# Four chained attention layers on 16 by 16 images: a new order of the stages in all four engine queues

## The chip, the core and the metric

The kernel runs on one core of a Trainium2 chip. TensorE (PE) multiplies and transposes, VectorE (DVE), ScalarE (ACT) and GpSimd (POOL) work elementwise, SyncE (SP) issues transfers. Each engine takes its own queue in program order and waits for the others by semaphores. The metric is device microseconds of one launch.

## What is computed

The input `x` has 2 batches of 128 channels of 16 by 16 pixels (N = 256), in float32. Four layers follow one another; batches never mix. Cut to what matters:

```python
# layer 0: group norm, attention over pixels
hn = group_norm(x); q, k, v = wq@hn + bq, wk@hn + bk, wv@hn + bv
x = wp @ (softmax(q.T @ k * C**-0.5) applied to v) + bp + x
# layer 1: position attention, then channel attention
pam = gamma_pam * (softmax(q.T @ k) applied to v) + x
x = gamma_cam * softmax(max(cen) - cen) @ pam + pam      # cen = pam @ pam.T
# layer 2: 8 heads of 16, with a fixed embedding added to q and k
x = softmax(q.T @ k / 4) applied to v, @ Wout + bout + x
# layer 3: linear attention and feed-forward, norms over channels
f = chan_ln(x) * norm_g
q, k, v = [dwconv3x3(w @ f, dw) for each]
q = softmax(q, over the 16 of a head) * 16**-0.5; k = softmax(k, over pixels)
o = silu(q applied to (k @ v.T));  x = chan_ln(out_w @ o) * out_norm_g + x
x = ff_w2 @ (chan_ln(gelu(ff_w1 @ chan_ln(x))) * ff_g2) + x
```

## The kernel before

Everything stays in SBUF once loaded; a batch is one tile of 128 channels by 256 pixels, and where pixels must stand on the partitions it is two tiles of 128 (NT = 2). Each engine's program is a list of stages, small functions that take the batch `b`, called in an order written out by hand. Within layer 0 and 1 batch `b` uses PSUM banks 4b to 4b+3.

Layers 0 and 1: TensorE computes `q0_product`, `k0_product`, `scores0`, VectorE `max0`, ScalarE `exps0`, TensorE `p0_transposes`, `scale0` (it spreads the reciprocal sums of `sums0` over the partitions), `mix0`, and VectorE `x1_sum`. Layer 1 repeats this (`qk1_product`, `scores1`, ... `pam_sum`) and goes on with `pam_transposes`, `energy`, `energy_min`, `energy_exp`, `ce_transpose`, `co_product` and `x2_sum`. Between them lie products on the weights alone: `wg_mean` and VectorE's `centre_wg` make `wgc`, from which GpSimd makes the convolution's weights; `ff_mean_1`, `ff_mean_2` and `centre_ff_1`, `centre_ff_2` do the same for the feed-forward. `keep_clock(n, dst)` issues n products of zeros that nothing reads.

Layer 2 works in four groups (two per batch, `grp` 0 to 3) of four heads. For each: `group_scores` (TensorE, into four banks), `group_max` (VectorE, four reductions of 128 by 512), `max_transposes`, `shift_add`, `group_scores_T` (the scores again, transposed, with the maxima subtracted), four `head_exp` (ScalarE), `group_mix`, `mixed_evac`, `mixed_transposes`, `o2_norm`. Per batch `o2_transposes`, `o2_evac` and `x3_tokens` end the layer.

Layer 3, per batch: `x3_stats` (VectorE), a root, `f_scale`, `f_transposes`, `f_evac` and `shift_edges` (ScalarE, three shifted copies of f). From there three ways run side by side. The q way is 18 products `conv(j, first, last)` on TensorE (j is the half of the pixels, first to last the taps), then `q_max`, `q_exp`, `q_norm`, `q_transposes`. The k way is `k_1x1`, nine taps on VectorE (`k_taps_0`, `_3`, ...) and their maximum, `k_exp`, `ek_transposes`. The v way is `v_1x1`, nine scaled copies on ScalarE (`v_products`), eight additions on GpSimd (`v_sums`, line 251), each of which waits for the one two ahead of it or more, so that they run one behind the other, and `v_transposes`, `v3_evac`. Then `ctx_product`, `context`, `o3_product`, `o3_tanh`, `silu`, `y_products` (two products in one stage), `y_stats`, root 4, `x4_sum`, `x4_stats`, `x4_transposes`, `x4_evac`, `h_products`, root 5, `gelu`, `h_stats`, `h_transposes`, `hT_evac`, `ff_product`, root 6, `y_sum`, `y_transposes`, `y_evac`. All inverse roots (`root3` to `root6`, line 213) are made on GpSimd, in the same queue as the value sums. In the tail the order alternates: a stage of batch 0, one of batch 1 further ahead in the chain.

Of the kernel before, what the change touches and what calls it, by code (L numbers as in the profile page):

```python
# [4 lines left out]
NB = 2  # L5
# [3 lines left out]
NT = N // 128  # L9
# [33 lines left out]
def build(nc, x, pack_a, pack_b, pack_c, taps, out):  # L43
# [5 lines left out]
    with ExitStack() as ctx:  # L49
# [147 lines left out]
        def _(pool):  # L197
# [62 lines left out]
        def _(act):  # L260
# [63 lines left out]
            for stage, b in ((k0_evac, 0), (k0_evac, 1), (exps0, 0), (exps0, 1), (v0_evac, 0), (rb0_evac, 0), (v0_evac, 1), (p0T_evac, 1),  # L324
                             (rb0_evac, 1), (k1_evac, 0), (v1_evac, 0), (k1_evac, 1), (exps1, 0), (exps1, 1), (v1_evac, 1), (rb1_evac, 0),
                             (p1T_evac, 1), (rb1_evac, 1), (pamT_evac, 0), (pamT_evac, 1), (energy_exp, 0), (energy_exp, 1), (outwg_evac, 0)):
                stage(b)
# [116 lines left out]
            for stage, b in ((k2_evac, 0), (k2_evac, 1), (v2_evac, 0), (v2_evac, 1)):  # L444
                stage(b)
            for grp in range(NB * NG):
                for i in range(HG):
                    head_exp(HG * grp + i)
                    if i == 1 and 0 < grp <= NG:
                        mixed_evac(0, grp - 1)  # L450
            mixed_evac(1, 0)
            x3T_evac(0)
            mixed_evac(1, 1)
            f_scale(0)
            f_evac(0)
            o2_evac(1)
            for stage, b in ((shift_edges, 0), (v_products(0, 4), 0), (x3T_evac, 1), (f_scale, 1), (v_products(4, 6), 0), (f_evac, 1),
                             (shift_edges, 1), (v_products(6, TAPS), 0), (k_exp, 0), (v_products(0, 3), 1), (q_exp, 0),
                             (v_products(3, TAPS), 1), (ekT_evac, 0), (qT_evac, 0), (v3_evac, 0),
                             (k_exp, 1), (o3_tanh, 0), (q_exp, 1), (gelu_table, 1), (ekT_evac, 1), (x4_evac, 0), (qT_evac, 1), (v3_evac, 1),  # L460
                             (o3_tanh, 1), (gelu, 0), (hT_evac, 0), (x4_evac, 1), (gelu, 1), (y_evac, 0), (hT_evac, 1), (y_evac, 1)):
                stage(b)
# [3 lines left out]
        def _(dve):  # L466
# [196 lines left out]
            for stage, b in ((q0_evac, 0), (q0_evac, 1), (xb0_sum, 0), (xb0_sum, 1), (max0, 0), (max0, 1), (sums0, 0), (p0T_evac, 0),  # L663
                             (sums0, 1), (centre_outw, 0), (x1_sum, 0), (x1_sum, 1), (q1_evac, 0), (q1_evac, 1), (centre_wg, 0), (max1, 0), (max1, 1),
                             (xb1_sum, 0), (xb1_sum, 1), (sums1, 0), (p1T_evac, 0), (sums1, 1),
                             (pam_sum, 0), (pam_sum, 1),
                             (half_masks, 0), (centre_ff_1, 0), (energy_min, 0), (ce_scale, 0), (energy_min, 1), (ceT_evac, 0), (centre_ff_2, 0),
                             (ce_scale, 1), (ceT_evac, 1), (x2_sum, 0), (x2_sum, 1)):
                stage(b)
# [48 lines left out]
            def k_taps(b, first=0, last=TAPS):  # L718
# [121 lines left out]
            for stage, b in ((k_taps_0, 0), (x3_stats, 1), (k_taps_3, 0), (k_taps_6, 0), (k_taps_8, 0), (k_taps_0, 1), (q_max, 0), (k_sums, 0),  # L840
                             (k_taps_3, 1), (q_norm, 0), (k_taps_6, 1), (context, 0), (k_taps_8, 1), (q_max, 1), (silu, 0), (q_norm, 1),
                             (y_stats, 0), (k_sums, 1), (x4_sum, 0), (x4_stats, 0), (context, 1), (silu, 1), (h_stats, 0), (y_stats, 1),
                             (y_sum, 0), (x4_sum, 1), (x4_stats, 1), (h_stats, 1), (y_sum, 1)):
                stage(b)
# [3 lines left out]
        def _(pe):  # L848
# [103 lines left out]
            def keep_before_qk1(b):  # L952
                pe.wait_ge(s["rb0_d"], 1)
                keep_clock(1, bank[1])

# [78 lines left out]
            for stage, b in ((q0_product, 0), (k0_product, 0), (q0_product, 1), (k0_product, 1), (scores0, 0), (scores0, 1),  # L1034
                             (v0_product, 0), (v0_product, 1), (p0_transposes, 0), (scale0, 0), (p0_transposes, 1), (scale0, 1), (mix0, 0),
                             (mix0, 1),
                             (wg_mean, 0), (keep_before_qk1, 0), (qk1_product, 0), (v1_product, 0), (qk1_product, 1), (scores1, 0), (scores1, 1), (v1_product, 1),
                             (p1_transposes, 0), (scale1, 0), (p1_transposes, 1), (mix1, 0), (scale1, 1), (mix1, 1),
                             (pam_transposes, 0), (ff_mean_1, 0), (energy, 0), (pam_transposes, 1), (ff_mean_2, 0), (energy, 1),
                             (ce_transpose, 0), (embedding(0), 0), (co_product, 0), (outwg_transpose, 0),  # L1040
                             (ce_transpose, 1), (embedding(1), 0), (co_product, 1), (embedding(0), 1), (embedding(1), 1), (qk2, 0)):
                stage(b)

            def group_scores(grp):

                b, g = divmod(grp, NG)
# [322 lines left out]
```

## Time and profile before

| | us |
|---|---|
| median of 3 runs | 104.99 |
| lowest, highest | 103.88, 105.0 |
| the profiled execution | 103.97 |
| its span | 102.2 |
| busy: TensorE, VectorE, ScalarE, GpSimd | 79.7, 59.7, 45.7, 29.4 |

The span runs from the first to the last instruction recorded; the rest of the execution's time lies around it. A chain row says when a piece of the chain that ended last starts and how long it is; "issue" is time in which the engine waits for nothing that the profile shows. A float32 product is recorded as two passes, so x4 stands for two products. Idle time in front of an instruction is put down to what ended it.

### The profile page before, as it was taken

What the parts mean: (1) busy time and instruction counts of PE and PEld (TensorE: products, weight loads), DVE (VectorE), ACT (ScalarE), POOL (GpSimd) and SP (SyncE); (2) the same over time, 40 slices, a digit from 0 to 9 for tenths busy, and PEclk for the clock granted to TensorE, in tenths of its full rate; (3) what the DMA queues carried; (4) which work ended last, traced back from release to release, by engine and by line L of the source; (5) the groups of instructions that cost most, each with busy time, mean ns of one, the idle gap of its engine ahead of it and who ended that gap; (6) DMA issues with size and microseconds to landing.
All of it is one profiled execution on the core that took longest, in us unless ns stands there. A gap on an engine that the chain in (4) does not pass through costs nothing.

```text
span 102.2 us, 1618 instructions
## 1 busy us (share of the span) xinstructions
PE 79.7 (78%) x549; PEld 56.8 (56%) x551; DVE 59.7 (58%) x188; ACT 45.7 (45%) x123; POOL 29.4 (29%) x61
## 2 busy tenths in 40 slices
PE   5879999979997974769698996998547477919760
PEld 2328975747755753627355595996335263806440
DVE  1457777694685498486734399398496410943420
ACT  5003571494422265383765773997183212401511
POOL 7921500393008000000002045788003800052010
PEclk9999999999999999999999999999985556996699
DMA  1996000000000000000000000000000000000011
GB/s 54 280 385 270 7 0 0 0 6 0 3 0 0 0 3 0 0 6 0 0 0 6 0 0 0 0 6 3 0 0 0 3 0 0 0 0 0 12 39 51
DMA packets 1304, 2.91 MB, mean 28 GB/s; under 512 B 144, under 2 KB 784, under 8 KB 1296
## 3 DMA queue, kind: packets, MB, share of 16 engines
q1 hardware_dynamic: 1152, 2.68, 7.3%
q10 hardware_dynamic: 144, 0.13, 0.4%
q8 instruction: 4, 0.07, 0.3%
q14 instruction: 4, 0.03, 0.1%
HBM read 2.55 MB, written 0.26 MB: 27 GB/s over the span
## 4 chain that ended last, share of the span: by engine, by line
PE 49%; DVE 16%; issue 11%; POOL 9%; ACT 6%; DMA 5%; SPq 1%; POOLq 0%; DVEq 0%
DVE nmx L690 10%; POOL vacc L251 6%; DMA wa<-in_pack_a 5%; PE bank L1052 5%; PE bank L1216 4%; POOL rs L213 3%; PE bank L858 3%; PE bank L973 2%; PE bank L994 2%; PE bank L980 2%; PE bank L948 2%; PE bank L899 2%; PE bank L1060 2%; PE bank L866 1%; ACT vprod L384 1%
## 5 line engine op out<-in xcount | busy, mean ns | idle before, releaser
L213 POOL TENSOR_TENSOR rs<-ve,mhalf 128x2 f32<-128x2 f32 x8 | 5.5, 698 | 42.3 <-DVE ve L490 42.3
L251 POOL TENSOR_TENSOR vacc<-vacc,vprod 128x240 f32<-128x240 f32 (+1 forms) x16 | 10.5, 657 | 6.4 <-ACT vprod L384 4.7
L690 DVE TENSOR_REDUCE nmx<-bank 128x2 f32<-128x512 f32 x16 | 9.9, 685 | 3.5 <-PE bank L1052 3.5
L348 ACT ACTIVATE pT<-bank 128x512 f32<-128x512 f32 x16 | 8.5, 600 | 7.7 <-PE bank L1070 7.7
L1148 PE MATMUL bank<-convw,fsh 128*128 128x128 f32 x72 | 8.7, 275 | 0.0
L1148 PEld LDWEIGHTS bank<-convw,fsh 128*128 128x128 f32 x72 | 8.4, 192 | 0.1
L866 PE MATMUL bank<-warm 128*128 128x512 bf16 x15 | 5.8, 532 | 1.4 <-DVE warm L496 1.2
L384 ACT ACTIVATE vprod<-bank,wc 128x256 f32<-128x256 f32 x16 | 6.5, 497 | 0.0
L733 DVE SCALAR_TENSOR_TENSOR kacc<-bank,wc,kacc 128x240 f32<-128x240 f32 (+1 forms) x16 | 6.4, 451 | 0.0
L229 POOL TENSOR_TENSOR convw<-wgc,tapw 128x128 f32<-128x128 f32 x9 | 3.9, 464 | 7.9 <-DVE wgc L639 7.9
L1052 PE MATMUL bank<-km,qm 32*128 32x256 f32 x64 | 4.6, 400 | 0.7 <-ACT km L341 0.7
L1060 PE MATMUL bank<-wa,nmx 128*128 128x128 f32 x8 | 1.6, 286 | 4.2 <-DVE nmx L690 4.2
L267 ACT ACTIVATE p<-bank,nmax 128x256 f32<-128x256 f32 x8 | 3.7, 472 | 2.4 <-DVE nmax L494 2.4
L1070 PE MATMUL bank<-qa,km 32*128 32x256 f32 x64 | 4.3, 380 | 0.2 <-DVE qa L697 0.2
L1081 PE MATMUL bank<-pT,v 128*32 128x256 f32 x64 | 4.3, 385 | 0.0
L235 POOL TENSOR_SCALAR xb<-x,wa 128x256 f32<-128x256 f32 x2 | 2.3, 1148 | 6.8 <-DVE x L660 6.8
L866 PEld LDWEIGHTS bank<-warm 128*128 128x128 bf16 x17 | 2.1, 136 | 3.7 <-issue 2.2
L1216 PE MATMUL bank<-w1c,x 128*128 128x256 f32 x8 | 3.9, 645 | 0.3 <-ACT x L421 0.3
L341 ACT ACTIVATE km<-bank,kone,kmask 128x256 f32<-128x256 f32 x4 | 2.0, 558 | 4.6 <-PE bank L1025 4.6
L272 ACT ACTIVATE k<-bank,wa 128x256 f32<-128x256 f32 x2 | 0.9, 474 | 6.8 <-PE bank L885 6.8
L1060 PEld LDWEIGHTS bank<-wa,nmx 128*128 128x128 f32 x8 | 0.8, 140 | 5.7 <-ACT pT L348 4.8
L1052 PEld LDWEIGHTS bank<-km,qm 32*128 32x128 f32 x64 | 2.9, 184 | 1.7 <-issue 1.5
(207 smaller groups left out, 187.4 us busy)
## 6 DMA issues: line engine op xcount, KB each, us to landing
wc<-in_pack_c SPq DMA_DIRECT2D x1, 649.0 KB, 7.1
wb<-in_pack_b SPq DMA_DIRECT2D x1, 612.0 KB, 6.0
tapw<-in_taps SPq DMA_DIRECT2D x1, 576.0 KB, 8.0
wa<-in_pack_a SPq DMA_DIRECT2D x1, 320.0 KB, 5.0
out<-y SPq DMA_DIRECT2D x2, 128.0 KB, 1.7
x<-in_x ACTq DMA_DIRECT2D x1, 128.0 KB, 2.9
x<-in_x SPq DMA_DIRECT2D x1, 128.0 KB, 2.7
wa<-in_pack_a SPq DMA_DIRECT2D x1, 72.5 KB, 2.6
```

What stands on the lines that cost most here:

```text
L213: nc.gpsimd.tensor_tensor(dst, src, mhalf[:, 0:width], ALU.pow).then_inc(done, 1)
L251: nc.gpsimd.tensor_add(vacc[b][:, oy, ox], vacc[b][:, oy, ox], vprod[n - 1][b][:, iy, ix]).then_inc(s["vsum_d"], 1)
L348: nc.scalar.activation(pT2[u % PT2_RING][:, :, :], tiles(bank[SCORE_T_BANKS[u % HG]]), ACT.Exp).then_inc(s["e2_d"], 1)
L384: nc.scalar.activation(dst, LC[b][:, 0:N].rearrange("p (h w) -> p h w", h=H), ACT.Copy, scale=tap("vdw", *CENTRE_FIRST[n])).then_inc(s["vp ...
L690: nc.vector.tensor_reduce(nmx2[g][:, :, col:col + 1], tiles(bank[SCORE_BANKS[i]]), AX.X, ALU.max, negate=True).then_inc(s["max2_d"], 1)
L733: nc.vector.scalar_tensor_tensor(acc, k1x1[:, iy, ix], tap("kdw", dy, dx), acc, ALU.mult, ALU.add).then_inc(s["vec"], 1)
L866: nc.tensor.matmul(dst[:, :], warm[:, 0:128], warm[:, :], start=True, stop=True)
L1052: product = nc.tensor.matmul(tiles(bank[SCORE_BANKS[i]])[:, t, :], qm2[b][rows, g, t * 128:(t + 1) * 128], km2[b][rows, g, :], start=True, ...
L1060: last = nc.tensor.transpose(bank[SHIFT_BANK[grp]][:, t * 128:(t + 1) * 128], nmx2[grp % NG][:, t, :], ident)
L1070: product = nc.tensor.matmul(tiles(bank[SCORE_T_BANKS[i]])[:, t, :], km2[b][rows, g, t * 128:(t + 1) * 128], qa2[b][rows, g, :], start=Tru ...
L1148: product = nc.tensor.matmul(LA[b][:, j * C:(j + 1) * C], fsh[dx][b][:, row:row + H // NT, :].rearrange("p h w -> p (h w)"), convw[:, 3 * ...
L1216: last = nc.tensor.matmul(tiles(LD[b])[:, t, :], x4[b][:, t * 128:(t + 1) * 128], w1c[:, :], start=True, stop=True)
```

## The change

No arithmetic changes. The stages of all four queues stand in a new order, each queue now in one list. In a few places a stage is cut so that its parts can be placed: `k_max` comes out of the last k taps, `yg_products` out of `y_products`, `v_products` and `conv` are cut at other taps. Waits that stood between the calls of layer 2 go into the stages. `keep_before_qk1` (one product of zeros) and `keep_before_rb6` (three) go, and `keep_in_tail(2)` comes three times. The core of the diff:

```diff
-            for stage, b in ((root3, 0), (v_sums(1, 4), 0), (root3, 1), (v_sums(4, TAPS), 0), (v_sums(1, 6), 1), (root4, 0),
-                             (v_sums(6, TAPS), 1), (root5, 0), (root4, 1), (root6, 0), (root5, 1), (root6, 1)):
+            for stage, b in ((root3, 0), (v_sums(1, 3), 0), (root3, 1), (v_sums(3, TAPS), 0), (v_sums(1, TAPS), 1),
+                             (root4, 0), (root4, 1), (root5, 0), (root5, 1), (root6, 0), (root6, 1)):
...
+                             (mixed_evac_of(0), 1), (x3T_evac, 0), (f_scale, 0), (mixed_evac_of(1), 1), (f_evac, 0), (shift_edges, 0),
+                             (o2_evac, 1), (v_products(0, 8), 0), (x3T_evac, 1), (f_scale, 1), (f_evac, 1), (v_products(8, TAPS), 0),
+                             (shift_edges, 1), (k_exp, 0), (v_products(0, 3), 1), (q_exp, 0), (v_products(3, 4), 1), (ekT_evac, 0),
+                             (v_products(4, 5), 1), (v3_evac, 0), (v_products(5, TAPS), 1), (qT_evac, 0), (k_exp, 1), (q_exp, 1),
+                             (ekT_evac, 1), (v3_evac, 1), (o3_tanh, 0), (qT_evac, 1), (o3_tanh, 1), (gelu_table, 0), (x4_evac, 0),
+                             (x4_evac, 1), (gelu, 0), (gelu, 1), (hT_evac, 0), (hT_evac, 1), (y_evac, 0), (y_evac, 1)):
...
+                             (p0T_evac, 0), (sums0, 1), (centre_outw, 0), (x1_sum, 0), (x1_sum, 1), (q1_evac, 0), (q1_evac, 1),
+                             (xb1_sum, 0), (max1, 0), (max1, 1), (centre_wg, 0), (sums1, 0), (p1T_evac, 0), (xb1_sum, 1), (sums1, 1),
+                             (pam_sum, 0), (pam_sum, 1), (centre_ff_1, 0), (energy_min, 0), (centre_ff_2, 0), (ceT_evac, 0),
+                             (energy_min, 1), (ce_scale, 0), (x2_sum, 0), (ce_scale, 1), (ceT_evac, 1), (q2_evac, 0), (x2_sum, 1),
...
+            for stage, b in ((q0_product, 0), (k0_product, 0), (q0_product, 1), (k0_product, 1), (scores0, 0), (scores0, 1),
+                             (v0_product, 0), (v0_product, 1), (p0_transposes, 0), (scale0, 0), (p0_transposes, 1), (mix0, 0),
+                             (scale0, 1), (mix0, 1), (qk1_product, 0), (v1_product, 0), (qk1_product, 1), (scores1, 0), (scores1, 1),
+                             (wg_mean, 0), (p1_transposes, 0), (v1_product, 1), (scale1, 0), (p1_transposes, 1), (mix1, 0), (scale1, 1),
+                             (mix1, 1), (pam_transposes, 0), (ff_mean_1, 0), (energy, 0), (pam_transposes, 1), (ff_mean_2, 0),
+                             (embedding(0), 0), (ce_transpose, 0), (energy, 1), (co_product, 0), (embedding(1), 0), (ce_transpose, 1),
+                             (qk2, 0), (outwg_transpose, 0), (co_product, 1), (embedding(0), 1), (embedding(1), 1),
...
+                             (max_transposes_1, 1), (o2_transposes, 0), (scores_T_1, 1), (x3_tokens, 0), (mix_0, 1), (mix_1, 1),
+                             (mixed_transposes_of(0), 1), (f_transposes, 0), (mixed_transposes_of(1), 1), (v_1x1, 0), (o2_transposes, 1),
+                             (k_1x1, 0), (x3_tokens, 1), (conv(0, 0, TAPS), 0), (conv(1, 0, 3), 0), (f_transposes, 1), (conv(1, 3, 6), 0),
+                             (k_1x1, 1), (v_1x1, 1), (conv(1, 6, TAPS), 0), (conv(0, 0, 3), 1), (ek_transposes, 0), (conv(0, 3, 6), 1),
+                             (v_transposes, 0), (conv(0, 6, TAPS), 1), (conv(1, 0, 3), 1), (q_transposes, 0), (conv(1, 3, TAPS), 1),
+                             (ctx_product, 0), (ek_transposes, 1), (v_transposes, 1), (o3_product, 0), (ctx_product, 1),
+                             (q_transposes, 1), (y_products, 0), (o3_product, 1), (yg_products, 0), (y_products, 1), (yg_products, 1),
+                             (x4_transposes, 0), (keep_in_tail(2), 1), (h_products, 0), (keep_in_tail(2), 1), (x4_transposes, 1),
+                             (keep_in_tail(2), 1), (h_products, 1), (h_transposes, 0), (h_transposes, 1), (ff_product, 0), (ff_product, 1),
+                             (y_transposes, 0), (y_transposes, 1)):
```

GpSimd, in layer 3, from batch 1's sums to the end. L251 is a value sum (`vprod_1` is batch 1's product), L213 a root; `ve4_d` to `ve6_d` tell which norm it belongs to, `rs_0` or `rs_1` the batch.

```order
 L251 TENSOR_TENSOR vacc<-vacc,vprod_1 128x16x15 [waits vsum_d,vprod_d]
-L213 TENSOR_TENSOR rs_0<-ve_0,mhalf 128x2 [waits ve4_d]
 L251 TENSOR_TENSOR vacc<-vacc,vprod_1 128x15x15 [waits vsum_d,vprod_d]
 L251 TENSOR_TENSOR vacc<-vacc,vprod_1 128x240 [waits vsum_d,vprod_d]
 L251 TENSOR_TENSOR vacc<-vacc,vprod_1 128x15x15 [waits vsum_d,vprod_d]
+L213 TENSOR_TENSOR rs_0<-ve_0,mhalf 128x2 [waits ve4_d]
+L213 TENSOR_TENSOR rs_1<-ve_1,mhalf 128x2 [waits ve4_d]
 L213 TENSOR_TENSOR rs_0<-ve_0,mhalf 128x2 [waits ve5_d]
-L213 TENSOR_TENSOR rs_1<-ve_1,mhalf 128x2 [waits ve4_d]
+L213 TENSOR_TENSOR rs_1<-ve_1,mhalf 128x2 [waits ve5_d]
 L213 TENSOR_TENSOR rs_0<-ve_0,mhalf 128x2 [waits ve6_d]
```

The last three sums stood behind batch 0's root 4 and now stand ahead of it; the roots then come in pairs.

TensorE before, from batch 1's convolution (`convw,fsh_1`) to batch 1's context product. `ek`, `qn` and `vacc` are the transposes of k, q and v (no batch in the name: batch 0's first), `v_0,ekT` the context, `qT,cm` is `o3_product`.

```order
L1148 MATMUL bank<-convw,fsh_1 128x128 x9
L1184 MATMUL bank<-wa,qn 128x128 x2
L1163 MATMUL bank<-wa,vacc 128x128 x2
L1177 MATMUL bank<-v_0,ekT 128x128 x2
L1191 MATMUL bank<-qT,cm 128x256
L1170 MATMUL bank<-wa,ek 128x128 x2
L1197 MATMUL bank<-outwc,s_0 128x128 x2
L1202 MATMUL bank<-outwg,s_0 128x128 x2
L1184 MATMUL bank<-wa,qn 128x128 x2
L1209 MATMUL bank<-wa,x4T 128x128 x2
L1163 MATMUL bank<-wa,vacc 128x128 x2
L1177 MATMUL bank<-v_1,ekT 128x128 x2
```

The same stretch of TensorE in the changed kernel, where the line numbers differ (L1133 convolution, L1155 k, L1148 v, L1169 q, L1162 context, L1176 `o3_product`):

```order
L1133 MATMUL bank<-convw,fsh_1 128x128 x3
L1148 MATMUL bank<-wa,vacc 128x128 x2
L1133 MATMUL bank<-convw,fsh_1 128x128 x6
L1169 MATMUL bank<-wa,qn 128x128 x2
L1133 MATMUL bank<-convw,fsh_1 128x128 x6
L1162 MATMUL bank<-v_0,ekT 128x128 x2
L1155 MATMUL bank<-wa,ek 128x128 x2
L1148 MATMUL bank<-wa,vacc 128x128 x2
L1176 MATMUL bank<-qT,cm 128x256
L1162 MATMUL bank<-v_1,ekT 128x128 x2
```

Batch 0's transposes of v and q now lie between pieces of batch 1's convolution, and batch 1's transposes and context follow batch 0's at once, where before batch 0 had gone on to its x4.

TensorE in layer 1, from batch 0's last mix of layer 0 (`pT,v`) to batch 1's scores (`k_1,q_1`): `wg,wc` is `wg_mean`, `warm` a product of zeros, `x_0,wb` 64x256 `qk1_product`.

```order
L948 MATMUL bank<-pT_1,v_1 128x256 x2
L908 MATMUL bank<-wg,wc 128x384
L866 MATMUL bank<-warm 128x512
L959 MATMUL bank<-x_0,wb 64x256
L965 MATMUL bank<-wb,x_0 128x128 x2
L959 MATMUL bank<-x_1,wb 64x256
L973 MATMUL bank<-k_0,q_0 128x256 x2
L973 MATMUL bank<-k_1,q_1 128x256 x2
```

In the changed kernel:

```order
L939 MATMUL bank<-pT_1,v_1 128x256 x2
L946 MATMUL bank<-x_0,wb 64x256
L952 MATMUL bank<-wb,x_0 128x128 x2
L946 MATMUL bank<-x_1,wb 64x256
L960 MATMUL bank<-k_0,q_0 128x256 x2
L960 MATMUL bank<-k_1,q_1 128x256 x2
L899 MATMUL bank<-wg,wc 128x384
```

`wg_mean` moved behind the scores and the product of zeros is gone.

## Rows read from the trace of the kernel before

**Rows 1.** The profile page: busy times, granted clock in 40 slices, chain by line, one costly group.
```profile
PE 79.7 (78%) x549; PEld 56.8 (56%) x551; DVE 59.7 (58%) x188; ACT 45.7 (45%) x123; POOL 29.4 (29%) x61
...
PEclk9999999999999999999999999999985556996699
...
DVE nmx L690 10%; POOL vacc L251 6%; DMA wa<-in_pack_a 5%; PE bank L1052 5%; PE bank L1216 4%; POOL rs L213 3%; PE bank L858 3%; PE bank L973 2%; PE bank L994 2%; PE bank L980 2%; PE bank L948 2%; PE bank L899 2%; PE bank L1060 2%; PE bank L866 1%; ACT vprod L384 1%
...
L1148 PE MATMUL bank<-convw,fsh 128*128 128x128 f32 x72 | 8.7, 275 | 0.0
```

**Rows 2.** The chain in order of time, layer 1: start, length, what.
```profile
15.82 0.65 PE bank L908 x2
...
16.61 0.65 PE bank L959 x2
...
21.27 0.97 DVE xb L588 x2
...
31.78 0.88 PE bank L1025 x4
32.66 0.03 issue
...
33.39 1.20 PE bank L1052 x16
```

**Rows 3.** The chain, first round of layer 2.
```profile
34.60 2.50 DVE nmx L690 x4
```

**Rows 4.** The chain, value sums of layer 3.
```profile
59.04 0.47 ACT vacc L384
...
71.66 6.57 issue
78.27 0.70 POOL rs L213
...
80.57 0.62 POOL vacc L251
...
81.23 0.70 PE bank L1163 x2
```

**Rows 5.** Timeline of GpSimd from 50 us: start, length, instruction, idle before.
```profile
59.95 2.34 POOL L251 TENSOR_TENSOR vacc<-vacc,vprod 128x240 f32<-128x240 f32 x3 [3.60 <-ACT vprod L384]
...
64.05 7.61 POOL L251 TENSOR_TENSOR vacc<-vacc,vprod 128x225 f32<-128x225 f32 x10 [1.10 <-ACT vprod L384]
```

**Rows 6.** Windows of TensorE: stretch, length, busy, clock, DMA share, GB/s.
```profile
66.00:71.00 5.00, 4.57 (x40) 1.00 0.02 5
71.00:76.00 5.00, 2.35 (x13) 0.99 0.00 0
76.00:83.00 7.00, 4.39 (x16) 0.50 0.00 1
83.00:86.00 3.00, 3.00 (x10) 0.50 0.00 0
86.00:93.00 7.00, 3.83 (x26) 0.99 0.00 0
```

**Rows 7.** Timeline of TensorE: products of four passes in the tail.
```profile
75.98 1.19 PE L1197 MATMUL bank<-outwc,s 128*128 128x128 f32 x4 [0.38 <-DVE s L796]
...
87.71 0.61 PE L1197 MATMUL bank<-outwc,s 128*128 128x128 f32 x4
...
92.86 2.01 PE L1216 MATMUL bank<-w1c,x 128*128 128x256 f32 x4 [0.26 <-ACT x L421]
```

**Rows 8.** Timeline of VectorE: the statistics of batch 1's x4.
```profile
91.92 0.48 DVE L483 BATCH_NORM_STATS2 st<-x4T 128x6 f32<-128x128 f32 x2
```

**Rows 9.** The chain, its last piece.
```profile
99.68 0.38 ACT y L441
```

**Rows 10.** Timeline of ScalarE: the last four exponentials of layer 2.
```profile
52.05 2.06 ACT L348 ACTIVATE pT<-bank 128x512 f32<-128x512 f32 x4 [1.53 <-PE bank L1070]
```

More of the change, by code:

```diff
@@ L441, in y_evac @@
                 nc.scalar.activation(y[b][:, :], LB[b][:, 0:N], ACT.Copy).then_inc(s["y_d"], 1)
[L444 to L461, printed above, removed]
+            def head_exps(grp, first, last):
+                def stage(b):
+                    for i in range(first, last):
+                        head_exp(HG * (NG * b + grp) + i)
+                return stage
@@ L840, in _, with k_taps_3 @@
[L840 to L843, printed above, removed]
+            def k_taps_3(b):
+                k_taps(b, 3, 6)
@@ L1032, in v2_product @@
                 last.then_inc(s["v2_p"], 1)
[L1034 to L1042, printed above, removed]
             def group_scores(grp):
                 b, g = divmod(grp, NG)
+                if grp == 0:
+                    pe.wait_ge(s["x2_d"], NB)
+                    pe.wait_ge(s["outwg_w"], 1)
+                else:
+                    pe.wait_ge(s["max2_d"], HG * grp)
+                if grp >= 3:
+                    pe.wait_ge(s["oe2_d"], grp - 2)
                 pe.wait_ge(s["q2_d"], NG * b + g + 1)
@@ L1099, in o2_transposes, with keep_in_tail @@
                 last.then_inc(s["oT2_p"], 1)
[L1101 to L1113 removed]
+            def keep_in_tail(n):
+                return lambda b: keep_clock(n, LB[b][:, :])
             def x3_tokens(b):
@@ L1252, in _ @@
-            group_scores(2)
-            pe.wait_ge(s["e2_d"], HG)
-            group_scores_T(1)
-            pe.wait_ge(s["max2_d"], 2 * HG + 1)
-            group_mix(0)
-            pe.wait_ge(s["e2_d"], HG + 2)
-            max_transposes(2)
-            pe.wait_ge(s["oe2_d"], 1)
-            group_scores(3)
-            pe.wait_ge(s["e2_d"], 2 * HG)
-            group_scores_T(2)
-            pe.wait_ge(s["max2_d"], 3 * HG + 1)
-            group_mix(1)
-            pe.wait_ge(s["e2_d"], 2 * HG + 2)
@@ L1266, in _ @@
-            max_transposes(3)
-            mixed_transposes(0, 0)
-            mixed_transposes(0, 1)
-            pe.wait_ge(s["e2_d"], 3 * HG)
-            group_scores_T(3)
-            o2_transposes(0)
-            group_mix(2)
-            x3_tokens(0)
-            group_mix(3)
-            mixed_transposes(1, 0)
-            mixed_transposes(1, 1)
-            f_transposes(0)
-            o2_transposes(1)
-            k_1x1(0)
-            v_1x1(0)
-            x3_tokens(1)
-            for stage, b in ((conv(0, 0, TAPS), 0), (conv(1, 0, 3), 0), (f_transposes, 1), (conv(1, 3, TAPS), 0), (k_1x1, 1), (v_1x1, 1),
-                             (conv(0, 0, TAPS), 1), (ek_transposes, 0), (conv(1, 0, TAPS), 1), (q_transposes, 0), (v_transposes, 0),
-                             (ctx_product, 0), (o3_product, 0), (ek_transposes, 1), (y_products, 0), (q_transposes, 1), (x4_transposes, 0),
-                             (v_transposes, 1), (ctx_product, 1), (h_products, 0), (o3_product, 1), (h_transposes, 0), (y_products, 1),
-                             (ff_product, 0), (x4_transposes, 1), (y_transposes, 0), (h_products, 1), (keep_before_rb6, 1),
-                             (h_transposes, 1), (ff_product, 1), (y_transposes, 1)):
```

126 lines of the change are left out of this document (56 added, 70 removed).

## Prediction, made before the changed kernel was timed

> **What bounds the kernel now.** I read the profile page first, its busy shares and its summary of the chain [rows 1]. No engine is full: TensorE is busy 78% of the span, and the chain that ended last passes from engine to engine. So the order in the queues decides, and the question for each part is what a stage stands behind. The chain in order of time gives four stretches. (a) Up to the first scores of layer 2 at 33.39 us, TensorE works and is broken by short waits; the product `wg_mean` at 15.82 and one clock-keeping matmul stand ahead of `qk1_product` at 16.61 [rows 2]. (b) From 34.60 to about 50 us four groups go round in 4.2 us each: 2.50 of maxima on VectorE [rows 3], then transposes and scores (1.20 [rows 2]) on TensorE. (c) From 59.04 on GpSimd adds the sixteen shifted value products, one behind the other. It starts at 59.95 and has done thirteen by 71.66; then it stands 6.57 us, makes a root, and only then does the last three, which end at 81.18 [rows 4, 5]. It waits there for `root4` of batch 0, although the three products were ready: this is the greatest loss on the chain. (d) From `v_transposes(1)` at 81.23 to the end at 102.2, 21.0 us, batch 1's tail runs, queued among batch 0's steps [rows 4, 9]. The windows show that TensorE was granted its upper level (1.00, 2.4 GHz) to 75 us, the lower (0.50, 1.2 GHz) from 76 to 86, and the upper again for most of 86 to 93 [rows 6]. The same four passes take 1.19 us at the lower level and 0.61 at the upper [rows 7].
>
> The profiled execution took 103.97 us with a span of 102.2, so 1.77 lie around the span. The median of the runs shown is 104.99; the profiled one lies near their lowest, 103.88. The sum is made against 103.97.
>
> **The change, stretch by stretch.** All times below are on the clock of the kernel before, so that rows can be compared.
>
> (a) `wg_mean` goes behind `scores1`, and the keeping matmul goes. `qk1_product(0)` needs only the first `x1`, which is ready by 15.6; it starts at about 15.75 instead of 16.61 [rows 2]: 0.86. `centre_wg` and one `xb1_sum` no longer stand ahead of the reciprocal for which TensorE waits (0.97 for the two sums [rows 2]): about 0.3. `qk2(0)` goes ahead of `co_product(1)` and of batch 1's embeddings, so the scaling of K (32.66 to 33.39 is TensorE's gap for it [rows 2]) lies beside them: 0.73. `energy_exp(0)` ahead of `pamT_evac(1)` and the smaller swaps give about 0.25. `half_masks` moves to a place where VectorE waited for `scores0`: nothing, as long as pack B has landed by then; if not, up to the 0.4 of its own length and the rest of the transfer. Sum 2.15. Bounds: 0 (each swap uncovers another wait of equal length) and 2.9.
>
> (b) The order of maxima, transposes and scores within a round is kept, so its 4.2 us stay. The added waits (`max2_d`, `e2_d`, `oe2_d` inside the stages) are those that stood between the calls before. Behind the last maxima, VectorE does both `o2_norm(0)` before `shift_add(3)`, which holds `group_scores_T(3)` up by about 0.25, and so the last four exponentials, which run from 52.05 to 54.1 [rows 10], to 54.35. Against this `x3_tokens(0)` goes ahead of `group_mix(2)` (1.1 sooner, the length of that mix), and `v_1x1(0)` goes ahead of `k_1x1(0)`, `o2_transposes(1)` and `x3_tokens(1)`. The first value product moves from 59.04 [rows 4] to about 57.35: the last mix ends at 55.35, transposed f at 55.85, its evacuation at 56.25, the product at 56.75, and `shift_edges` and `o2_evac(1)` fill ScalarE to 57.35.
>
> (c) GpSimd takes the first sum at 58.2. Ten sums took 7.61 with their handovers [rows 5], so 0.76 each. Two sums to 59.7, `root3(1)` to 60.45, fourteen more sums at 0.76 to 71.1. ScalarE must deliver: it makes seven of batch 0's products at once, the ninth by 62.2, and batch 1's come between 64.1 and 68.1, each before its turn. `v3_evac(0)` stands among them and waits for the eighth sum, at 65.05, which TensorE transposes between two pieces of convolution; that is early enough, since batch 1's fifth product is wanted only at 68.1. So the sums end at 71.1 instead of 81.18 [rows 4]: 10.1, of which 6.57 is the wait, 0.70 the root, 1.75 the earlier start and 1.1 a wait for products that stood before the ten [rows 5]. What is late next: nothing on GpSimd; `root4` finds the engine free, since batch 0's statistics now end some 3 us behind the sums. Bound from below: if ScalarE is late by one blocked evacuation, 2 us less; from above, 11.
>
> (d) Behind the sums both batches now go in step. Priced at the upper level for batch 1: transposes 0.3, queue of `o3_product(0)` 0.45, context 0.5, q transposes 0.2, wait for batch 0's silu and y products to 2.15, `o3_product(1)`, tanh and silu to 3.6, y products to 4.2, statistics (0.48 for the two, plus the aggregates: 0.95 in all [rows 8]) and batch 0's `x4_stats` ahead of its own, x4 at 6.65, transposes, evacuation and two keeping matmuls to 7.65, `h_products` 0.9 (the same four passes as `qk2`, 0.88 [rows 2]), gelu to 9.4, transposes and evacuation to 10.5, ff 1.1 to 11.6, y sums, transposes and the copy of 0.38 to 13.1, then 2.1 to the end of the span as before [rows 9]: 15.2. At the lower level throughout, every product doubles (1.19 against 0.61, and `h_products` 2.01 [rows 7]) and the six keeping matmuls stand in the way as well: 24. I take 17.5: TensorE will be idle for about 1.7 of the 2.3 us ahead of the tail, and before the level fell behind a stretch with 2.35 busy of 5 [rows 6], so I expect it to fall once; but at the lower level the lockstep tail keeps TensorE occupied, as it was without a break from 83 to 86 before the level rose [rows 6]. So some 3 us of products are paid double. Gain 21.0 − 17.5 = 3.5; bounds 5.8 and −3.
>
> The Trainium skill, TensorE: Matmul & The Clock Gate, section "HAM oscillation — how this bites in real kernels", says that waits between bursts bring the throttle back each time. By that rule the tail, which waits several times, would stay near the lower level; that is the first rival, and by it alone the sum would be 94.9. The trace agrees that the level falls behind idle stretches [rows 6].
>
> **Sum.** 2.15 + 10.1 (with the start of (b) in it) + 3.5 = 15.75, less 0.2 for the two stores that now leave together: 15.6. 103.97 − 15.6 = 88.4 us.
>
> **Rivals.** (1) *The clock stays low through the tail.* Stretch (d) takes 24: 88.4 + 6.5 = 94.9; with a late recovery about 92. For it: the idle ahead of the tail. Against: in the kernel before, a dense spell brought it back [rows 6]. Chance 0.22 for 91 to 95. (2) *The queues bind elsewhere.* ScalarE's blocked evacuation or VectorE's k taps hold the products back (2 us) or the first stretch gives nothing (2.15): 90.5 to 93. Chance 0.13. (3) *Slower than before.* In each attention round TensorE waits for the 2.50 of maxima [rows 3]; with the keeping matmul ahead of it gone, the level could fall there already and stay low. The four rounds then cost 6.4 more (1.6 of TensorE each: the scores of 1.20 and two transposes), the convolutions 8.5 (72 passes of busy 8.7 [rows 1]), the products between them about 3, and the tail is 24 and not 15.2: 26.7 on top of 86.1, the sum with the tail at the upper level, so 113. It decides once the level falls before the third round. Against: in the slices of these rounds the grant was 0.9 or more before [rows 1], with the same gaps, and the matmul stood 17 us ahead of them [rows 2]. Chance 0.02. (4) *The change does not do what it says*, GpSimd still waits, for a product instead of the root: then the sums end near 79 and the time is about 97 to 100. The order of the queue is fixed by the code and the products are ready; chance 0.03.
>
> **The numbers.** My forecast (86 to 91) has 0.60, rivals (1) 0.22, (2) 0.13, (4) 0.03, (3) 0.02. The range 85.5 to 94 takes the forecast with the tail wholly at the upper level (86.1) and most of rivals (1) and (2); left out are some 0.15. A measurement can tell about 2% from no change; every case but (3) is below 102.9, so faster 0.96, same 0.02, slower 0.02.
>
> **What would show it.** Right: the chain has no wait of several us on GpSimd; sixteen sums and one root in one run of about 13 us that ends near 69 (2.1 earlier than on the clock above); first scores of layer 2 near 31.2; four rounds of 4.2; `v_transposes(1)` near 69.2; both batches' roots in pairs; the end 15 to 20 behind the sums. Wrong: first scores still at 33 (stretch (a)); gaps between sums with ScalarE as releaser (c); a grant of 0.50 from the sums to the end (d); gelu of batch 0 waiting behind `x4_evac(1)` for longer than batch 1's own chain.

## The result, and the profile after

The changed kernel takes 89.73 us (median of 4 executions, 88.63 to 89.98), the kernel before 104.44 (103.12 to 105.0). The ratio is 0.863, with a 95% interval of 0.847 to 0.880; it leaves disturbed executions out. The profiled execution took 89.75 with a span of 88.0. The forecast was 88.4 with a span of 86.6.

The page of the changed kernel: busy times, granted clock in 40 slices, and the chain by engine.

```profile
PE 76.4 (87%) x553; PEld 55.1 (63%) x553; DVE 59.6 (68%) x188; ACT 46.0 (52%) x123; POOL 30.0 (34%) x61
...
PEclk9999999999999999999999999999999957999999
...
PE 56%; DVE 25%; ACT 7%; POOL 5%; issue 4%; POOLq 0%; ACTq 0%
```

The same work fills a larger share of a shorter span (TensorE 87%, 78% in [rows 1]). The granted clock dips in two slices of forty; before it was below 0.9 in seven [rows 1]. GpSimd's queue from the last stretch of layer 2 to the end of the sums, as a timeline; it answers to [rows 5]:

```profile
57.01 1.51 POOL L251 TENSOR_TENSOR vacc<-vacc,vprod 128x240 f32<-128x240 f32 x2 [3.72 <-ACT vprod L380]
58.62 0.70 POOL L213 TENSOR_TENSOR rs<-ve,mhalf 128x2 f32<-128x2 f32 x1
59.28 11.13 POOL L251 TENSOR_TENSOR vacc<-vacc,vprod 128x240 f32<-128x240 f32 x14
```

Two sums, a root, and fourteen sums without a wait. The chain in order of time, from the first scores of layer 2 to the end of the sums and on into the tail; it answers to [rows 2, 4, 9]:

```profile
31.69 1.16 PE bank L1036 x16
...
65.31 0.38 ACT vprod L380
...
65.70 0.70 POOL vacc L251
...
69.81 0.62 POOL vacc L251
...
70.47 0.69 PE bank L1148 x2
...
79.73 1.15 PE bank L1202 x4
...
80.95 0.84 ACT h L428 x2
81.80 0.50 ACT hT L433
...
82.34 2.07 PE bank L1212 x16
...
85.46 0.38 ACT y L437
```

The 6.57 us of [rows 4] are gone from the chain. `v_transposes(1)` starts at 70.47 instead of 81.23. The chain holds only the last six sums: at 65.70 a sum starts just as ScalarE's product for it is ready, and ahead of that the chain runs through VectorE's k taps and ScalarE. So the sums without a gap and the way that feeds them are of nearly one length here. TensorE's windows show one fall of the level, from about 70 to 74 us:

```profile
69.00:70.00 1.00, 0.11 (x1) 0.00 (x0) 0.90 (x6) 0.53 (x2) 0.86 (x2) 1.00 0.00 0
70.00:72.00 2.00, 1.53 (x5) 1.13 (x6) 0.69 (x1) 0.38 (x1) 0.41 (x1) 0.62 0.00 0
72.00:74.00 2.00, 2.00 (x12) 1.94 (x11) 0.77 (x2) 0.77 (x2) 0.00 (x0) 0.53 0.00 0
74.00:76.00 2.00, 1.42 (x11) 1.21 (x10) 1.28 (x7) 1.37 (x2) 0.70 (x1) 1.00 0.00 0
```

The columns are the stretch, its length, the busy times of TensorE, its weight loads, VectorE, ScalarE and GpSimd, and then the granted clock, DMA share and GB/s.

### The profile page after: what moved, and what is told of

Same layout as the page of the kernel before. It is cut to its first block, busy times and chain, and to the rows that moved or that the text cites. A ratio compares the mean times of both kernels' runs of the same rounds, so it can differ in the third digit from the quotient of the medians.

```text
span 88.0 us, 1629 instructions
## 1 busy us (share of the span) xinstructions
PE 76.4 (87%) x553; PEld 55.1 (63%) x553; DVE 59.6 (68%) x188; ACT 46.0 (52%) x123; POOL 30.0 (34%) x61
## 4 chain that ended last, share of the span: by engine, by line
PE 56%; DVE 25%; ACT 7%; POOL 5%; issue 4%; POOLq 0%; ACTq 0%
DVE nmx L683 11%; PE bank L857 6%; PE bank L1036 5%; POOL vacc L251 5%; DVE kacc L726 4%; PE bank L849 3%; PE bank L1202 3%; PE bank L1212 2%; PE bank L939 2%; PE bank L960 2%; PE bank L967 2%; PE bank L890 2%; ACT pT L344 2%; PE bank L1182 2%; PE bank L1048 1%
## 5 line engine op out<-in xcount | busy, mean ns | idle before, releaser
L213 POOL TENSOR_TENSOR rs<-ve,mhalf 128x2 f32<-128x2 f32 x8 | 5.6, 697 | 29.0 <-DVE ve L490 28.9
L251 POOL TENSOR_TENSOR vacc<-vacc,vprod 128x240 f32<-128x240 f32 (+1 forms) x16 | 10.8, 676 | 5.6 <-ACT vprod L380 3.7
L1133 PE MATMUL bank<-convw,fsh 128*128 128x128 f32 x72 | 9.0, 275 | 0.0
L1133 PEld LDWEIGHTS bank<-convw,fsh 128*128 128x128 f32 x72 | 8.6, 192 | 0.1
L857 PE MATMUL bank<-warm 128*128 128x512 bf16 x19 | 7.0, 497 | 1.2 <-DVE warm L496 1.2
L483 DVE BATCH_NORM_STATS2 st<-bank 128x6 f32<-128x128 f32 x8 | 2.0, 289 | 2.6 <-PE bank L1107 1.7
L1063 PEld LDWEIGHTS bank<-qa,km 32*128 32x128 f32 x64 | 3.2, 185 | 0.3 <-DVE qa L690 0.2
```

The costliest lines, as they stand in the source:

```text
L213: nc.gpsimd.tensor_tensor(dst, src, mhalf[:, 0:width], ALU.pow).then_inc(done, 1)
L251: nc.gpsimd.tensor_add(vacc[b][:, oy, ox], vacc[b][:, oy, ox], vprod[n - 1][b][:, iy, ix]).then_inc(s["vsum_d"], 1)
L857: nc.tensor.matmul(dst[:, :], warm[:, 0:128], warm[:, :], start=True, stop=True)
L1063: product = nc.tensor.matmul(tiles(bank[SCORE_T_BANKS[i]])[:, t, :], km2[b][rows, g, t * 128:(t + 1) * 128], qa2[b][rows, g, :], start=Tru ...
L1133: product = nc.tensor.matmul(LA[b][:, j * C:(j + 1) * C], fsh[dx][b][:, row:row + H // NT, :].rearrange("p h w -> p (h w)"), convw[:, 3 * ...
```

## The experiments

**Where the gain comes from.** The first four kernels each take one part of the change. They ran on one chip; the kernel before had a median of 104.56 there (13 executions).

`e_pool_only`, the kernel before with this edit:

```diff
-(root3, 1), (v_sums(4, TAPS), 0), (v_sums(1, 6), 1), (root4, 0), (v_sums(6, TAPS), 1), (root5, 0)
+(root3, 1), (v_sums(4, TAPS), 0), (v_sums(1, TAPS), 1), (root4, 0), (root5, 0)
```

> The kernel before with one part of the change: GpSimd's queue alone, all of batch 1's value sums ahead of root4 of batch 0. My theory: the 6.57 us wait goes and the sums end near 73.9 us instead of 81.2, but TensorE's queue still has x4_transposes(0) (79.4) ahead of v_transposes(1), so v_transposes(1) moves only from 81.2 to about 80.1 and the time falls by about 1 us (ratio 0.99). Rival: the wait on GpSimd is the loss by itself; then v_transposes(1) comes near 75 to 76 and the time falls by 5 to 7 us (ratio 0.93 to 0.95).

Measured: median 103.53, ratio 0.988 (0.971 to 1.006), not to be told from no change (the interval allows up to 3 us). At equal mean clock it is 102.2 and 103.01 against 103.03 and 103.16 (0.93). GpSimd and TensorE, from the two timelines:

```profile
65.06 10.04 POOL L251 TENSOR_TENSOR vacc<-vacc,vprod 128x225 f32<-128x225 f32 x13 [1.10 <-ACT vprod L384]
```

```profile
80.76 0.74 PE L1209 MATMUL bank<-wa,x4T 128*128 128x128 f32 x2 [0.96 <-DVE x4T L807]
81.29 0.63 PE L1163 MATMUL bank<-wa,vacc 128*128 128x128 f32 x2
```

The thirteen sums run through and end at 75.10, and `v_transposes(1)` (L1163) still starts at 81.29, because it stands behind `x4_transposes(0)` (L1209), which waits for VectorE. (The profiled execution had lost about 1 us in layer 2, so all its times are that much later.) The wait of 6.57 us was on the chain, but taken away alone it handed the chain to TensorE's queue, which was late by nearly as much.

`e_follow`, the same and, in the tail, batch 1's steps moved forward:

```diff
-(ctx_product, 0), (o3_product, 0), (ek_transposes, 1), (y_products, 0), (q_transposes, 1), (x4_transposes, 0),
-(v_transposes, 1), (ctx_product, 1), (h_products, 0), (o3_product, 1), (h_transposes, 0), (y_products, 1),
+(ctx_product, 0), (o3_product, 0), (ek_transposes, 1), (v_transposes, 1), (y_products, 0), (q_transposes, 1),
+(ctx_product, 1), (x4_transposes, 0), (o3_product, 1), (h_products, 0), (y_products, 1), (h_transposes, 0),
...
-(ekT_evac, 1), (x4_evac, 0), (qT_evac, 1), (v3_evac, 1),
+(ekT_evac, 1), (v3_evac, 1), (qT_evac, 1), (x4_evac, 0),
...
-(y_stats, 0), (k_sums, 1), (x4_sum, 0), (x4_stats, 0), (context, 1), (silu, 1), (h_stats, 0), (y_stats, 1), (y_sum, 0), (x4_sum, 1)
+(y_stats, 0), (k_sums, 1), (x4_sum, 0), (context, 1), (x4_stats, 0), (silu, 1), (y_stats, 1), (h_stats, 0), (x4_sum, 1), (y_sum, 0)
```

> The kernel before with GpSimd's sums ahead of root4(0), and on TensorE, ScalarE and VectorE only batch 1's v transposes, context product and o3_product moved forward in the tail, so that batch 1 follows its sums; everything up to the convolution as before. My theory (the wait is worth its length only when the queues behind it follow): v_transposes(1) near 75.5 instead of 81.2, 4 to 5 us less than before (ratio 0.95 to 0.96), more than four times what the GpSimd order alone gives. Rival: batch 0's steps, now behind batch 1's, hold up the end, and it gives no more than GpSimd's order alone.

Measured: median 97.4, ratio 0.937 (0.927 to 0.947): 6.5 us less, more than expected. TensorE's timeline:

```profile
75.78 0.38 PE L1163 MATMUL bank<-wa,vacc 128*128 128x128 f32 x2
...
87.59 1.04 PE L1216 MATMUL bank<-w1c,x 128*128 128x256 f32 x4
```

`v_transposes(1)` is 5.4 us earlier. The remaining gain goes with the level: batch 1's `h_products` take 1.04 at the upper level here and 2.01 at the lower in [rows 7], and the level was low from 77.3 to 84.1 here where it had been low from 75.9 to 86.1 and again from 93.0 to 96.4. No run held the level up in the kernel before, so how much of the 6.5 us is the shorter path and how much the level stays open. The order of the other queues can't be tried without GpSimd's: with `v_transposes(1)` ahead of `y_products(0)`, and the last three sums behind `root4(0)`, each would wait for the other for ever.

`e_head`, the kernel before with the changed kernel's lists of layers 0 and 1 on TensorE, VectorE and ScalarE, up to the first scores of layer 2 (and, just behind them, `v2_product(0)` ahead of `qk2(1)`):

> The kernel before with the new order of layers 0 and 1 (up to the first scores of layer 2) on all engines, the rest as before. In the changed kernel the first scores started 1.70 us earlier than before. My theory: the stages behind move as a block, so this kernel gives 1.7 us (ratio 0.984), with first scores near 31.7. Rival: the gain is lost or grows behind it, because the level of TensorE's clock in the tail changes with the shift; then the time moves by less than 0.7 or more than 2.7.

Measured: ratio 0.985 (0.978 to 0.991), 1.6 us less by the ratio, and TensorE's timeline has the first scores at 31.59. `e_after_old_head`, the changed kernel with the old lists there:

> The changed kernel with the old order of layers 0 and 1. If the stretches add up: 14.2 us less than before without the 1.7 of the head, so about 12.5 less (ratio 0.88), first scores at 33.4, sums ending near 72.1. Rival (the head's order is needed for the later gain, since an idle queue there feeds layer 3): less than 11 us.

Measured: median 91.85, ratio 0.876 (0.859 to 0.893); the sums end at 73.2. By the ratios the two parts add up to the whole within the intervals: 1.5% and 12.4% against 13.7%. The sums end about 1 us later than expected, and the level of TensorE had fallen once in layer 2 (0.58 from 42 to 45 us), which lengthens that stretch by as much.

**The clock.** `c_after`, `e_fill`, `e_nokeep` and `e_unchunk` ran on one chip, the other kernels from here on, `c_after_2` among them, on another.

> The changed kernel again, on the same chip as the next three, for comparison: 0.863 of the kernel before, 89 to 90 us.

Measured: median 89.5, ratio 0.849 (0.842 to 0.855). Its six executions fall into two lots: 88.34, 88.50 and 88.54 with a mean clock of 1.00, and 90.46, 90.60 and 90.69 with 0.96. The profiled one was of the first lot. Its windows for TensorE alone (stretch, length, busy time and count of the matmuls, then the granted clock, DMA share and GB/s), and the end of its sums and of its chain:

```profile
69.00:70.00 1.00, 0.00 (x0) 1.00 0.00 0
70.00:72.00 2.00, 1.60 (x10) 1.00 0.00 0
72.00:74.00 2.00, 1.86 (x12) 1.00 0.00 0
```

```profile
69.61 0.62 POOL vacc L251
...
84.24 0.38 ACT y L437
```

So with the same program and the same idle stretch of 1.36 us before `v_transposes(1)`, the level fell in one execution and not in another. From the end of the sums to the end of the span it is 16.5 us here (70.23 to 86.7), and 17.6 with one fall (70.42 to 88.0); in the profile of `c_after_2`, where the level fell from 71.9 to 75.3, it is 17.3. A fall in the tail costs about 1 us.

`e_fill` puts clock-keeping matmuls into TensorE's wait:

```diff
-(ctx_product, 0), (ek_transposes, 1), (v_transposes, 1), (o3_product, 0), (ctx_product, 1),
+(ctx_product, 0), (keep_in_tail(2), 1), (ek_transposes, 1), (keep_in_tail(6), 1), (v_transposes, 1), (o3_product, 0), (ctx_product, 1),
```

> The changed kernel with eight more clock-keeping matmuls (two ahead of ek_transposes(1), six ahead of v_transposes(1)) where TensorE waits for VectorE, ScalarE and GpSimd from 68 to 70.4 us. Theory: the idle there is what makes the granted level fall to 0.50 from about 70.7 to 74; with it filled the level stays at 1.00, the products of the lockstep tail cost half, and the time falls by 1 to 1.7 us (88 to 88.6). Rival: the level falls all the same, or the fillers push v_transposes(1) back by as much as they save: within 0.3 us of the changed kernel or slower.

Measured: median 89.07, three executions at 88.4 to 88.6 (clock 1.00) and three at 89.6 (0.98), none at 0.96. By the ratio (0.855, 0.849 to 0.862) it is not to be told from the changed kernel. It looked as if one of two falls was gone; the other had to be elsewhere. The profile of `e_unchunk` (below) shows where it can be, in the second round of layer 2:

```profile
38.00:40.00 2.00, 0.75 (x6) 0.93 0.00 0
40.00:42.00 2.00, 2.00 (x24) 0.50 0.04 8
42.00:44.00 2.00, 2.00 (x32) 0.72 0.00 0
```

There TensorE waits for the second round's maxima. No profile of the changed kernel itself caught a fall in this place; that its executions at 0.96 fell twice is inferred from their mean clock and time. `e_fill_all` is `e_fill` with two, four and two keeping matmuls ahead of the first three `max_transposes`, into a bank whose last reader is waited for:

```diff
+(keep_in_rounds(2, s["v2_d"], NG), 0), (max_transposes_0, 0),
...
+(keep_in_rounds(4, s["e2_d"], 1), 0), (max_transposes_1, 0),
...
+(keep_in_rounds(2, s["e2_d"], HG + 1), 0), (max_transposes_0, 1),
```

> The changed kernel once more, for comparison on the same chip: 88.4 us in executions where TensorE keeps its upper level throughout, about 1 us more for each fall of the level (in the rounds of layer 2 near 40 us, in the tail near 70 us).

> The changed kernel with clock-keeping matmuls in both places where the granted level was seen to fall: the eight of the run before ahead of batch 1's transposes, and two, four and two into TensorE's waits for the maxima in the first three rounds of layer 2. Theory: every execution keeps the upper level, so all lie at 88.3 to 88.7 us, median about 1 us below the changed kernel's, and the spread of 2 us shrinks to 0.4. Rival: falls come whatever TensorE does in these waits; then the median and the spread stay as they are (89.5, 88.3 to 90.7).

Measured on one chip: the changed kernel 88.98 (six executions, 88.22 to 90.81, clocks 0.959 to 0.999), `e_fill_all` 88.62 (five executions, 88.53 to 88.69, clocks 0.997 to 1.00). The spread fell from 2.6 us to 0.16. The median gained 0.36 beside this run, and not the full 1: in half of the changed kernel's executions nothing falls, and there the fillers gain nothing and may cost some 0.2 (88.22 to 88.50 without them). The two ratios to the kernel before, 0.858 (0.852 to 0.864) and 0.856 (0.852 to 0.860), overlap. Chance is an unlikely reason for the five steady executions: of the changed kernel's sixteen in all, seven had a mean clock of 0.99 or more, and five such in a row would come about once in sixty times. So this version is steadier than the changed kernel rather than faster. Its windows:

```profile
38.00:40.00 2.00, 1.61 (x10) 1.00 0.00 0
40.00:44.00 4.00, 3.66 (x55) 1.00 0.02 4
68.00:70.00 2.00, 1.86 (x9) 1.00 0.00 0
70.00:74.00 4.00, 3.70 (x22) 1.00 0.00 0
```

`e_nokeep` takes the three `keep_in_tail(2)` out of the changed kernel:

> The changed kernel without the six clock-keeping matmuls around h_products. Theory: they lie under the copies of ScalarE and cost at most 0.3 us, and without them TensorE is so little busy from 76 to 80 that the level falls in h_products, h_transposes or ff_product: slower by 1 to 2.5 us. Rival: they only fill idle time, the level stays, and the time is the same or 0.3 less.

Measured: median 88.91, 88.40 to 90.59, ratio 0.851 (0.844 to 0.857). The theory fell and the rival held: the executions that kept the upper level took 88.40 to 88.44 without the six matmuls and 88.34 to 88.54 with them. In the profiled execution the level stood at 1.00 from 76 to 80 without them.

**The convolution in pieces.** `e_unchunk`, the changed kernel with batch 0's transposes behind batch 1's whole convolution:

```diff
-(conv(0, 3, 6), 1), (v_transposes, 0), (conv(0, 6, TAPS), 1), (conv(1, 0, 3), 1), (q_transposes, 0), (conv(1, 3, TAPS), 1),
+(conv(0, 3, 6), 1), (conv(0, 6, TAPS), 1), (conv(1, 0, 3), 1), (conv(1, 3, TAPS), 1), (v_transposes, 0), (q_transposes, 0),
```

> The changed kernel with one part undone: batch 0's v and q transposes behind batch 1's whole convolution, not between its pieces. Theory: ScalarE stands in v3_evac(0) until about 67.8, four of batch 1's value products come about 3 us later, GpSimd waits about 0.5 to 1.5 us for them, and the time grows by that (90 to 91.3). Rival: the sums have enough products in hand and the time stays within 0.3.

Measured: six executions at 88.74 to 91.0, median 90.51 against 89.5; five of them had a lower clock (0.96 to 0.97). The two timelines, ScalarE and GpSimd:

```profile
68.25 0.38 ACT L400 ACTIVATE v<-bank 128x256 f32<-128x256 f32 x1 [2.09 <-PE bank L1148]
68.53 1.56 ACT L380 ACTIVATE vprod<-bank,wc 128x256 f32<-128x256 f32 x4
```

```profile
60.41 7.85 POOL L251 TENSOR_TENSOR vacc<-vacc,vprod 128x240 f32<-128x240 f32 x10
69.07 3.02 POOL L251 TENSOR_TENSOR vacc<-vacc,vprod 128x240 f32<-128x240 f32 x4 [0.81 <-ACT vprod L380]
```

The mechanism is as expected: ScalarE stands 2.09 us in `v3_evac(0)` with four of batch 1's products behind it, and GpSimd waits 0.81 for the first of them. From the first to the last sum it is 13.97 us, against 13.4 in the changed kernel. The one execution near the upper level took 0.2 to 0.4 more (88.74 against 88.34 to 88.54). So this part of the change is worth some 0.2 to 0.6 us; the rest of the 1.0 between the medians is falls of the level, and whether the order causes them more often six executions can't tell.

**What binds now.** `e_fewsums` leaves out the last four of batch 1's eight value additions, so part of the value path isn't computed (`v_transposes(1)` waits for four sums less):

```diff
-(v_sums(3, TAPS), 0), (v_sums(1, TAPS), 1),
+(v_sums(3, TAPS), 0), (v_sums(1, 5), 1),
```

> The changed kernel without the last four of batch 1's eight value additions (part of the output is left out), so that GpSimd ends 3.2 us sooner. Theory: GpSimd's sums bound the stretch to 70.4, but batch 1's q and k come only 1.5 to 2 us before them, so the time falls by 1.2 to 2 us of the 3.2 (near 86.8 to 88). Rival 1: the sums are the only bound and it falls by 3.2. Rival 2: VectorE's queue (q_norm(1) ahead of silu(0)) is the bound already and it falls by less than 0.5.

Measured: median 87.2; the profiled execution has a span of 85.3 at clock 1.00, against 86.7 in `c_after`: 1.4 of 3.2 (on its own chip 86.9 to 87.26 against 88.22 to 88.50 of `c_after_2`, at the upper level). Its chain:

```profile
65.61 1.18 DVE kacc L726 x3
...
68.65 0.42 ACT eq L386
69.07 0.31 ACT ekT L396
69.37 0.28 ACT v L400
```

VectorE's queue (k taps, maxima of k and q) takes the place of the sums. Two chains of nearly one length run to 70 us now.

**The weight product in layer 1.** `e_wg_back`, with `wg_mean` ahead of `qk1_product(0)` again, behind batch 1's mix (`pT_1,v_1`):

> The changed kernel with wg_mean back ahead of qk1_product(0), everything else as changed. Theory: qk1_product(0) waits for the 0.65 of that product, and most of it arrives at the first scores of layer 2: 0.5 to 0.65 later (about 32.1), the time 0.5 to 0.7 more. Rival: another wait of layer 1 takes it up and the first scores move by less than 0.2.

Measured: median 90.48, ratio 0.875 (0.869 to 0.880). Executions with a clock of 0.98 took 90.03, 90.34 and 90.61, where the changed kernel's took 89.45 and 89.50: 0.5 to 1.2 more. On the chain, from batch 0's mix of layer 0 to the first scores:

```profile
13.55 1.06 PE bank L939 x4
...
15.70 0.65 PE bank L899 x2
...
31.93 1.07 PE bank L1036 x15
```

That is 18.38 us, and 17.88 in the changed kernel (13.81 to 31.69): 0.50, as expected; in `c_after` and `c_after_2` it is 17.87 and 17.86. (The mix itself begins at 13.5 to 13.8 in these profiles, so the stretch tells more than the start of the scores.)

## Why the prediction was right, point by point

The time saved in the profiled execution is 14.2 where I forecast 15.6: 1.70 in (a), 9.1 in (b) and (c) together (81.18 to 70.42, less the 1.70), 3.4 in (d).

**(a) Layers 0 and 1.** Forecast 2.15, measured 1.70 by the two profiles (33.39 to 31.69) and 1.6 by `e_head`. Over all profiles with this order and `wg_mean` in its new place, nine of them, the first scores start at 31.35 to 31.69, and at 33.39 to 33.46 in the four with the old one: 1.7 to 2.1. The total holds; of the steps `e_wg_back` shows one, 0.50 for `wg_mean`, and the others have no run of their own. Part of what is missing is a term that I did not have: GpSimd makes the convolution's weights later now, and VectorE's two additions of `pam` fall beside it. They take longer than the 0.42 each that they took before:

```profile
23.73 0.64 DVE L609 TENSOR_TENSOR pam<-t,xb 128x256 f32<-128x256 f32 x1
...
24.85 0.53 DVE L609 TENSOR_TENSOR pam<-t,xb 128x256 f32<-128x256 f32 x1
```

The first of them is on the chain, 0.22 us. `half_masks` has no row on the chain in its new place, as said.

**(b) Layer 2.** The rounds kept their 4.2 us (maxima at 32.85, 37.05, 41.22, 45.39). The first value product started at 56.09. The forecast, moved by the measured head, was 55.65. The late 0.45 is in one place: ScalarE's queue has `o2_evac(1)` ahead of `v_products(0)`, and I took its input as ready. It stood 0.54 for it:

```profile
55.81 0.38 ACT L354 ACTIVATE o<-bank 128x256 f32<-128x256 f32 x1 [0.54 <-PE bank L1094]
56.09 0.47 ACT L380 ACTIVATE vacc<-bank,wc 128x256 f32<-128x256 f32 x1
```

**(c) The sums.** One run with no wait, from 57.01 to 70.42, as forecast; ScalarE delivered in time. It took 13.4 where I had 12.9: a sum with its handover took 0.795 (14 in 11.13) and not 0.76. That term is mis-sized: ten sums of one stretch were my sample, and the groups by shape show the wider form at 716 ns where it had 680. Two of the eight wide sums ran beside VectorE's additions of `kc` and took 0.81 and 0.74; the handover itself is there since each sum but a batch's first waits for the one just before it.

```profile
L251 POOL TENSOR_TENSOR vacc<-vacc,vprod 128x240 f32<-128x240 f32 x8 | 5.7, 716 | 4.4 <-ACT vprod L380 3.7
L251 POOL TENSOR_TENSOR vacc<-vacc,vprod 128x225 f32<-128x225 f32 x8 | 5.1, 637 | 1.1
```

Most important is a statement that I made only in passing, that the queues behind the sums must go in step. My sum booked 10.1 us for (c) and 3.5 for (d) as if each stood alone. `e_pool_only` shows that taking away the 6.57 us wait alone gives about 1 (medians 1.0 apart, not told from nothing), and `e_follow` that with the tail's queues behind it the two are worth 6.5. The total held because the whole order was changed.

**(d) The tail.** Forecast 17.5 from the end of the sums, less 0.2 for the stores; measured 17.6. Two errors cancel, which is luck. First, at the upper level (`c_after`) the tail takes 16.5 and not 15.2. By its chain batch 1's `y_products` end 4.9 us behind the sums where I had 4.2, and `h_products` take 1.13 to 1.15 where `qk2` gave 0.88; why, no run tells. The largest step is the feed-forward, 2.07 on the chain where I had 1.1: ScalarE's list has `hT_evac(0)` behind `gelu(1)`, so batch 0's `ff_product` starts only then and its eight passes stand ahead of batch 1's eight. The transposes and the evacuation in front of it gave 0.6 back. Second, the one fall that I expected costs about 1, not 2.3. The 0.2 for the stores did not show: from the end of the last copy to the end of the span it is 2.1 us in both kernels. The expectation itself, that the level falls at the head of the tail and comes back, is what the profiled execution shows (0.62 and 0.53 from 70 to 74, then 1.00). The other executions show that it is no certainty.

**The rivals.** (1), a low clock through the tail, did not come: the level returned by 74 us, and none of the changed kernel's sixteen executions was above 90.81. The rule of the Trainium skill (TensorE: Matmul & The Clock Gate, "HAM oscillation — how this bites in real kernels") tells of longer waits, for transfers, in another kernel. It holds as to the direction, since both places where the level fell lie behind waits. A repeated fall within one tail was not seen in the changed kernel. It was in the kernel before, where the level fell a second time behind an idle stretch of 2.08 us at 89.7 (TensorE's windows):

```profile
93.00:97.00 4.00, 3.54 (x10) 0.58 0.01 2
```

My reading of that kernel's tail stopped at 93 us and left this fall out, although the 2.01 by which I priced `h_products` lies in it. (2), other queues bind, came in part: 0.45 of ScalarE in (b) is of that kind. (3) came as a short event, not as a state: the level can fall in the second round of layer 2, and it is back by 43 to 46.3 us. It was seen there in kernels with the old order of layers 0 and 1 (`e_after_old_head`, `e_pool_only`) and with the new (`e_unchunk`, `e_wg_back`, `e_head`). The old order has the keeping matmul, so its removal isn't the cause. (4) did not come.

## What to carry to other kernels

A wait on the chain is worth its length only as far as the queues behind it can follow: before pricing it, ask on each engine which instruction stands ahead of the one that it frees, and when that one is ready. Here the 6.57 us of waiting gave about 1 us alone, which the runs can't tell from nothing, and 6.5 with three other queues moved. And when two chains of nearly equal length run side by side, as the value sums and the k and q ways do now, time one of them away before shortening it: four sums less, 3.2 us of work, gave 1.4.

## What the runs showed of the hardware

The granted level of TensorE differs between executions of one program: of six executions of the changed kernel three had a mean of 1.00 and three 0.96, and lay 2.1 us apart. The idle stretch ahead of the tail (68 to 70.4 us, at most 1.36 us without a break) ended in a fall in one execution of the changed kernel and not in another. The one at 38 to 40 us ended in a fall in `e_unchunk` and not in the changed kernel's profiles, up to there the same program. With matmuls of zeros in both stretches the spread was 0.16 us in five executions, and they may cost some 0.2 (88.62 against a median of 88.39 where nothing falls); the same matmuls where ScalarE's short copies were the only wait did nothing that could be told.

A VectorE instruction with two inputs in SBUF and a GpSimd addition lengthen each other. `pam` adds two tiles in SBUF; `t`, just ahead of it, has one input in PSUM, and GpSimd makes the convolution's weights beside both. `t` keeps its 0.42 and `pam` takes 0.64 (0.53 for batch 1), against 0.42 in the kernel before, where GpSimd had done:

```profile
23.27 0.42 DVE L605 TENSOR_TENSOR t<-bank,rb 128x256 f32<-128x256 f32 x1 [1.08 <-PE bank L981]
```

The addition of `kc` (both inputs in SBUF) shows it from both sides. In `e_pool_only` it starts while a value sum runs and takes 0.78; in the kernel before it falls into a gap of GpSimd's and takes 0.42:

```profile
74.59 0.78 DVE L738 TENSOR_TENSOR kc<-kacc 128x256 f32<-128x256 f32 x1
```

```profile
73.59 0.42 DVE L738 TENSOR_TENSOR kc<-kacc 128x256 f32<-128x256 f32 x1
```

In the changed kernel the sums start while it runs, it keeps its 0.42, and they take 0.81 (batch 0) and 0.74 (batch 1) where the same shape takes 0.69 to 0.71:

```profile
L251 POOL TENSOR_TENSOR vacc<-vacc,vprod x16: 606/680/810, 57.0 to 69.8; 128x240 f32<-128x240 f32 x8, 128x225 f32<-128x225 f32 x8
```

(Duration in ns: shortest, median, longest.) So in the pairs with `kc` the one that starts second pays. In the kernel before no sum took more than 0.704. The Trainium skill, GPSIMD Engine Reference, section "Key points", says that GpSimd shares its SBUF interfaces with VectorE and names VectorE instructions with two SBUF inputs as a case of contention; these rows agree with it.
